# Fetching the rows of the attention heads quad by quad, and making the key parts two steps later

## The reference

```python
q = _apply_rope_full(x @ wq.T); k = _apply_rope_full(x @ wk.T); v = x @ wv.T
scores = jnp.einsum('bhqd,bhkd->bhqk', q, k) / math.sqrt(Dh)
scores = scores + _alibi_slopes(H)[None, :, None, None] * rel[None, None]
scores = jnp.where(causal[None, None], jnp.float32(-1000000000.0), scores)
out = jnp.einsum('bhqk,bhkd->bhqd', jax.nn.softmax(scores, axis=-1), v)
return out.transpose(0, 2, 1, 3).reshape(B, S, D) @ out_w.T + out_b
```

## Time and profile before

| | |
|---|---|
| median of 3 runs | 1346.04 us |
| the profiled execution | 1347.82 us |
| its span (first to last instruction) | 1346.0 us |
| mean granted clock of PE | 0.958 |
| busy: PE, DVE, ACT, POOL | 1223.6, 908.5, 641.6, 235.5 us |
| a_q loads of 512 KB, issue to landing | 4.2 us (8 of them) |
| a_k loads of 256 KB, issue to landing | 5.2 us (16 of them) |

### The profile page before, as it was taken

The page is one execution under the profiler, slowest core; times in us unless marked ns, Lnnn a source line. Parts: engine busy times, 40 slices in busy tenths (PEclk is TensorE's granted clock), DMA queues, the critical chain, the costliest instruction groups (busy, mean ns, idle before and its releaser), DMA issues.

```text
span 1346.0 us, 17205 instructions
## 1 busy us (share of the span) xinstructions
PE 1223.6 (91%) x6152; PEld 794.7 (59%) x6152; DVE 908.5 (67%) x1754; ACT 641.6 (48%) x1183; POOL 235.5 (17%) x201
## 2 busy tenths in 40 slices
PE   5998788899899889799999979789998997989998
PEld 3676444567666555466667744346676664556665
DVE  6765856455467698987765677564555677989765
ACT  4544344534323487862234325444433226969322
POOL 3001000000020065661000010000000101928210
PEclk9999879999999979799999999899999997979999
DMA  6213121000101121220200032200001012212120
GB/s 225 56 32 95 41 57 35 2 1 0 63 1 63 42 69 35 95 95 0 72 24 0 24 88 54 61 4 1 1 1 63 13 51 57 79 57 79 64 71 9
DMA packets 32581, 63.20 MB, mean 47 GB/s; under 512 B 4176, under 2 KB 19824, under 8 KB 32304
## 3 DMA queue, kind: packets, MB, share of 16 engines
q1 hardware_dynamic: 32496, 62.11, 14.7%
HBM read 54.16 MB, written 8.45 MB: 47 GB/s over the span
## 4 chain that ended last, share of the span: by engine, by line
PE 70%; DVE 12%; ACT 9%; DMA 3%; POOL 2%; issue 2%; SPq 1%; DVEq 0%; ACTq 0%; POOLq 0%
PE bank L1519 13%; PE bank L1520 12%; PE bank L1521 12%; PE bank L1688 9%; PE bank L1528 5%; PE bank L1834 3%; DVE a_mx L1400 3%; ACT n_part L1067 3%; PE bank L1597 3%; PE bank L1749 2%; PE bank L1658 2%; ACT n_da L1059 2%; POOL n_hc L819 2%; DMA a_k<-stack_dram 2%; PE bank L1724 2%
## 5 line engine op out<-in xcount | busy, mean ns | idle before, releaser
L1244 DVE SCALAR_TENSOR_TENSOR f_hl<-bank,f_hh 128x512 fp32r<-128x512 f32 x192 | 131.8, 689 | 130.4 <-ACT f_hh L893 129.7
L893 ACT ACTIVATE f_hh<-bank 128x512 fp32r<-128x512 f32 x192 | 114.7, 598 | 188.8 <-PE bank L1597 188.4
L955 ACT ACTIVATE m_sl<-bank 128x512 f32<-128x512 f32 x144 | 86.1, 599 | 235.2 <-PE bank L1521 234.8
L819 POOL TENSOR_TENSOR n_hc<-n_h,n_cs 128x512 f32<-128x512 f32 x128 | 159.9, 1278 | 179.0 <-DVE n_h L1490 172.6
L1519 PE MATMUL bank<-xT_h,mw_h 128*128 128x512 f32 x288 | 161.3, 560 | 3.5 <-DVEq L529 2.7
L1490 DVE TENSOR_TENSOR_SCAN n_h<-n_da,bank 128x512 f32<-128x512 f32 x128 | 149.9, 1207 | 10.0 <-PE bank L1528 7.2
L1688 PE MATMUL bank<-m_h,mw 128*128 128x512 f32 x288 | 145.6, 594 | 0.0
L1400 DVE TENSOR_REDUCE a_mx<-bank 128x1 f32<-128x384 f32 (+3 forms) x176 | 106.2, 637 | 52.6 <-PE bank L1789 50.2
L1311 DVE TENSOR_TENSOR m_t<-m_sl,bank 128x512 f32<-128x512 f32 x128 | 87.9, 687 | 78.4 <-PE bank L1521 77.3
L1834 PE MATMUL bank<-n_hc,ident 128*128 128x512 f32 x256 | 136.1, 619 | 0.2
L973 ACT ACTIVATE a_p<-bank 128x1024 f32<-128x1024 f32 (+3 forms) x128 | 87.8, 703 | 91.7 <-PE bank L1726 90.7
(11 more groups left out here) (241 smaller groups left out, 2362.7 us busy)
## 6 DMA issues: line engine op xcount, KB each, us to landing
n_cs<-c_dram SPq DMA_DIRECT2D x32, 512.0 KB, 3.6
m_c<-comb_dram SPq DMA_DIRECT2D x28, 512.0 KB, 5.1
a_q<-stack_dram SPq DMA_DIRECT2D x8, 512.0 KB, 4.2
a_k<-stack_dram SPq DMA_DIRECT2D x16, 256.0 KB, 5.2
stage_fw<-in_fw_dram SPq DMA_DIRECT2D x6, 512.0 KB, 7.0
stack_dram<-R SPq DMA_DIRECT2D x16, 192.0 KB, 2.8
w_stage<-in_mw_dram SPq DMA_DIRECT2D x9, 256.0 KB, 2.7
stack_dram<-R SPq DMA_DIRECT2D x16, 128.0 KB, 2.6
```

What stands on the lines that cost most here:

```text
L819: n_hcs.by(nc.gpsimd.tensor_tensor(n_hc[:, i % 4, :], n_h[:, i % 4, :], n_cs[:, j % C_RING, i // 2 % 2, :], ALU.mult))
L1244: f_lo.by(V.scalar_tensor_tensor(f_h[1][:, i % 4, :], bank[:, i % 3, :], 0.0, f_h[0][:, i % 4, :].bitcast(F32), ALU.max, ALU.subtract))
```

## The change

There are now three groups of transfers for the rows of the heads: the first half as before (group 0), the third quad (group 1) and the fourth quad (group 2), each with semaphores of its own. Every group is one load of queries and two of keys. In the first batch's unit SP fetches group 0 of the next batch behind the scores of step 15, then waits for the scores of step 23 (the third quad's last) and fetches group 1; group 2 comes behind step 31. Ahead of a stage the load of group 0's queries follows the key rows instead of going before them. On PE the first slot of the fourth quad waits for group 2. Inside the first batch's steps, stages 15 and above come two later: the key parts on ACT at steps 11, 12 and 13, the residuals on DVE at 11 and 12.

```diff
+KEYS_LATER = 2
@@ stage_at
+                if host == "mha":
+                    ahead = {n + KEYS_LATER * (n >= 15): name for n, name in ahead.items()}
                 return ahead.get(i)
@@ sync engine
-            def half_queries(k, n):
-
-                sp.wait_ge(a_wr.sem, a_wr.at(k, 5))
-                pairs = slice(4 * n, 4 * n + 4)
-                a_ldq[n].by(sp.dma_start(a_qs[n][:], stack_dram[0].rearrange("o r h t -> (o r) h t")[:, pairs]))
-
-            def half_keys(k, n):
-
-                sp.wait_ge(a_wr.sem, a_wr.at(k, 11))
-                pairs = slice(4 * n, 4 * n + 4)
-                for odd in range(2):
-                    a_ldk[n].by(sp.dma_start(a_ks[n][64 * odd:64 * odd + 64, odd::2], stack_dram[1, odd][:, pairs]))
+            def head_rows_in(k, n):
+
+                first, count = ((0, 4), (4, 2), (6, 2))[n]
+                to = slice(first % 4, first % 4 + count)
+                sp.wait_ge(a_wr.sem, a_wr.at(k, 5))
+                a_ldq[n].by(sp.dma_start(a_qs[first // 4][:, to],
+                                         stack_dram[0].rearrange("o r h t -> (o r) h t")[:, first:first + count]))
+                sp.wait_ge(a_wr.sem, a_wr.at(k, 11))
+                for odd in range(2):
+                    a_ldk[n].by(sp.dma_start(a_ks[first // 4][64 * odd:64 * odd + 64, odd::2][:, to],
+                                             stack_dram[1, odd][:, first:first + count]))
@@
-                        half_queries(k, 1)
-                        half_keys(k, 1)
+                        head_rows_in(k, 1)
+                        head_rows_in(k, 2)
                     for quad in range(QUADS):
                         if p == 0 and quad == 3:
 
                             sp.wait_ge(a_s2.sem, a_s2.at(k, NS2 // 2 - 1))
-                            half_queries(k + 1, 0)
-                            half_keys(k + 1, 0)
+                            head_rows_in(k + 1, 0)
+
+                            sp.wait_ge(a_s2.sem, a_s2.at(k, 3 * STEPS_4 - 1))
+                            head_rows_in(k + 1, 1)
                         sp.wait_ge(a_mok.sem, a_mok.at(k, quad))
@@
                             sp.wait_ge(a_s2.sem, a_s2.at(k - 1, NS2 - 1))
-                            half_queries(k, 1)
-                            half_keys(k, 1)
+                            head_rows_in(k, 2)
@@
-                    half_queries(k, 0)
                     head_rows(k, 1)
-                    half_keys(k, 0)
+                    head_rows_in(k, 0)
@@ tensor engine
-                    if n % (2 * NS1) == 0:
-                        rows_of_half(k, quad // 2)
+                    if n % NS1 == 0 and quad != 1:
+                        rows_of_quads(k, max(quad - 1, 0))
```

More of the change, by code:

```diff
@@ L438, in program @@
         a_wr = sig("a_wr", "mha", 12, 16)
-        a_ldq = [sig(f"a_ldq_{n}", "mha", 1, 16) for n in range(2)]
-        a_ldk = [sig(f"a_ldk_{n}", "mha", 2, 16) for n in range(2)]
+        a_ldq = [sig(f"a_ldq_{n}", "mha", 1, 16) for n in range(3)]
+        a_ldk = [sig(f"a_ldk_{n}", "mha", 2, 16) for n in range(3)]
         a_rld = sig("a_rld", "pair", 1, 16)
@@ L583, in head_rows @@
                 if k % 2 == 1:
-                    for n in range(2):
+                    for n in range(3):
                         sp.wait_ge(a_ldq[n].sem, a_ldq[n].at(k - 1, 0))
@@ L1751, in weigh_heads, with rows_of_quads @@
                 a_pv.by(ins)
-            def rows_of_half(k, n):
-                pe.wait_ge(a_fill.sem, a_fill.at(k // 2, 2 * n + 1))
+            def rows_of_quads(k, n):
+                pe.wait_ge(a_fill.sem, a_fill.at(k // 2, 1 if n == 0 else 3))
                 pe.wait_ge(a_ldq[n].sem, a_ldq[n].at(k, 0))
```

## The result

The changed kernel takes 1352.09 us, the median of 8 runs (1349.38 to 1355.25); the kernel before takes 1345.99 us in 8 runs (1345.21 to 1348.04). The ratio is 1.0041 with a 95% interval of 1.0032 to 1.0051: slower by 6.1 us. The profiled execution took 1352.11 us, with a span of 1350.3 us against 1346.0.

What follows compares the result with a forecast made beforehand. TensorE was taken as the bound, busy 1223.6 of 1346.0 us. Key parts −4.1, split −6.9, third quad's rows +16.4 make +5.4 us: 1351.4 us against the median of 1346.04, range 1345.5 to 1357 (own range 1348.5 to 1355).

Steps and rivals of the forecast that it cites:

- The signs that the prediction named: Step 24 idle 5 to 7 us, clock near 0.5 behind it; key stops 2 to 3 us; second half's stop gone.
- Third quad's rows behind step 23: SP's new wait ahead of the fourth quad's maxima: step 24 6.0 us later plus 2.2 slow clock, 16.4 us lost in all.
- the lower bound of 1.0 us: Bound for SP's one a_q and two a_k issues behind step 23, if half size issues faster; 1.7 was taken.
- The write behind the bulk: The small max_dram write behind the 512 KB rows is held up: 2.5 us until its loads, against 1.34 with an empty queue.
- The rival with a write not held up: At step 24 the max_dram write isn't delayed by the rows: 4.8 us lost per pair; total 1346.8 us, chance 0.16.
- Clock: PE's clock falls behind each new stop at step 24, costing 2.2 us more per pair, bounds 0 and 4.4.
- mostly paid back: Write not held up at step 24, slow phase 1.1 us on average: 11.8 lost, 11.0 gained, 1346.8 us; chance 0.16.
- Key parts: Two steps later, the stop between steps 8 and 16 goes: 2.8 us gained in pair 1, 1.3 in pair 2, together 4.1.
- The split: Fourth quad's rows alone behind step 31: stop for the second half goes, 2.46 us in pair 1, 4.46 in pair 2, together 6.9.
- Queries behind the key rows: Ahead of the stage, the first a_q load behind the six key-row writes: cost 0, bound 0.5 us per pair.
- the bulk is no faster for being half: Write ahead of step 24 waits nearly 7 us: 8.7 at step 24, 2.7 more per pair, 1356.8 us; chance 0.15.
- faster: PE's clock holds behind the key stop and at step 24: 15.4 gained, 9.6 lost, 1340.2 us; chance 0.12.

Runs made afterwards that it cites:

- experiment 1: Changed kernel with the wait for step 23 and the third quad's rows moved behind the fourth quad's maxima transfers: 1333.93 us, ratio 0.9912 to the kernel before.
- experiment 3: Changed kernel without the wait for step 23, third and fourth quad's rows both fetched behind step 31 in two groups: 1333.15 us.
- experiment 4: Changed kernel with the key parts back at their old steps: 1355.38 us.
- experiment 2: Changed kernel with the wait for step 23 left in place, the third quad's transfers issued behind the fourth quad's maxima: 1341.54 us.
- Experiment 7: Kernel of experiment 1 with the key parts one step later instead of two: 1334.24 us.
- experiment 6: Kernel of experiment 3 with the key parts at their old steps, so the split alone: 1340.62 us.
- Experiment 8: Kernel of experiment 1 with the first queries fetched ahead of the key rows again: 1334.37 us.

## Why the prediction was right, and what it had wrong

Forecast 1351.4, measured 1352.1. The mechanism is shown by more than the agreement of the sum: with the wait and its rows moved behind the two loads (experiment 1), the stop at step 24 is gone in both pairs and with it 18 us. The signs that the prediction named came too, the nearest to a miss being step 8 to 24 in pair 1, 32.1 us against its 33.3. That the total is 0.7 us off is partly luck: by the experiments the three terms are −5.7 (−3.3 within the change), −5.4 and +18.2, where the sum had −4.1, −6.9 and +16.4. (Its chances don't quite add up: 0.53 and 0.15 make 0.68, not 0.70.)

- **Third quad's rows behind step 23.** The forecast was 16.4 us. By rows it is 6.15 + 5.86 of stops and 1.85 + 1.57 of slow clock, 15.4; by the medians of the change and experiment 1 it is 18.2 (by the ratios 17.4), with about 2.4 us either way from the two intervals. The pieces: handover 0.31 (said 0.24), issues 1.64 (1.7), write 3.06 and 2.77 (2.5), loads to matmul 2.86 (3.15). The write was 0.3 to 0.6 us longer than said, the way from the loads to the matmul 0.3 shorter; these errors cancel. Half the bytes did not halve the issue time: two a_k issues of half size last 1.22 us against 1.28, so the lower bound of 1.0 us was no real case.
- **The write behind the bulk.** The Trainium skill ("DMA: Bandwidth & Descriptors", section "Queues, rings and completion order") has descriptors of one DMA engine consumed in order, and the semaphore's increment land only after that engine's earlier writes. The trace agrees: the write's loads could be issued 4.70 us after the bulk's first issue (191.78 to 196.48), where a group of that size takes 4.7 to 5.5 us by experiment 3; the changed kernel's 16 a_k loads of 128 KB land 3.6 us after their issue (median), which would be 196.4 for the last one here (an estimate from 192.77 + 3.6). All four writes right behind the rows took 2.75 to 3.06 us (the change and experiment 4), the two at the same place with nothing ahead 1.36 and 1.35 (experiment 2). The rival with a write not held up falls. The prediction's own evidence was weaker than it read: its 2.47 us followed the bulk, but in the same trace the write at 203.22 took 2.20 us (its loads went out at 205.42) with nothing issued for 10 us ahead of it. So how much of the 2.8 to 3.1 us the bulk makes is shown for this place alone: 1.4 to 1.7.
- **Clock.** It fell behind both new stops, worth 1.85 and 1.57 us, not 2.2. The rival "mostly paid back" had this at 1.1 us and the write not held up: the slow phases came out halfway between the two, the write was held up in full.
- **Key parts.** Forecast 4.1 us; 5.7 measured alone, 3.3 within the change. The stop between steps 8 and 16 went as said, its 3.39 us. In the trace, pair 1 gained 1.2 us more than forecast and pair 2 0.7 less, which cancel in part. Three things were off. Step 8 to 24 in pair 1 is 32.1 us, 1.2 under my 33.3, which I had from pair 2 with its slow phase: in the changed kernel's pair 1 the slow phase behind the keys is half as long. Its windows (184.13 and 847.16 are the first slots behind the keys):

```profile
184.30:187.70 3.40, 3.40 (x23) 1.48 (x22) 1.33 (x2) 0.00 (x0) 0.00 (x0) 0.57 0.02 5
187.70:191.00 3.30, 2.99 (x30) 1.58 (x28) 2.26 (x5) 1.19 (x2) 0.00 (x0) 1.00 0.00 0
...
846.50:853.30 6.80, 6.12 (x36) 3.27 (x36) 2.22 (x4) 1.15 (x2) 0.00 (x0) 0.53 0.00 0
```

  And a stop of 1.45 us that I hadn't named appears at 172.62, as VectorE waits 2.20 us for the second key part behind the values. Experiment 7 speaks against its costing anything. Timelines of ACT and then of DVE, changed kernel, pair 1:

```profile
166.80 0.64 ACT L885 ACTIVATE R<-xn 128x512 bf16<-128x512 f32 x1
...
170.12 0.60 ACT L998 ACTIVATE a_vs<-bank 128x512 f32<-128x512 f32 x1 [0.80 <-PE bank L1523]
170.61 0.62 ACT L885 ACTIVATE R<-xn 128x512 bf16<-128x512 f32 x1
```

```profile
171.27 0.69 DVE L1388 TENSOR_TENSOR xn<-xn,R 128x512 f32<-128x512 f32 x1 [2.20 <-ACT R L885]
```

  The first key part waits no longer (3.25 us in the earlier trace rows), as said. In pair 2 the change gave 0.6 instead of 1.3 us: the third quad's maxima, whose write had taken 1.34 us, took 2.45 (831.59 to 834.04), and held the key rows behind them.
- **The split.** Forecast 6.9 us, measured 5.4 alone. The stop for the second half went as said; a part of the 5.4 comes from the shorter stop between steps 8 and 16, which the prediction didn't have (experiment 6). Step 24 to the output takes 26.61 us without stops (experiment 1) against the 26.28 expected, 0.3 per pair of the difference, and the arrangement without the early wait keeps a third-quad stop of about 1 us (experiment 3); the interval of the ratio is 1.8 us either way.
- **Queries behind the key rows.** Said 0, at most 0.5 per pair. The stage of the changed kernel starts 3.04 and 2.71 us behind the start of the last matmul group ahead of it (128.38 to 131.42, 790.98 to 793.69), before 2.51 and 2.50 (128.93 to 131.44, 789.71 to 792.21): 0.5 and 0.2 later. Experiment 8 finds no gain from undoing it.

Of the two rivals on size, "the bulk is no faster for being half" falls by experiment 3 (4.7 to 5.5 us, not 6.9), and "faster" by the granted clock of 0.52 behind step 24.

Open: key stops differ between profiled executions whose program is the same up to there (2.29 and 3.09 us in the change, 1.18 and 1.70 in experiment 1, 1.95 and 1.70 in experiment 3), so 1.3 and 2.5 us of the difference between the change and experiment 1, which lie between steps 8 and 24, may be chance; one profile each can't tell. The changed kernel's runs also scatter more (5.9 us) than those before (2.8), with no cause found.

## What to carry to other kernels

In a queue that runs in order, ask of every wait that you add what stands behind it and when that is due: here a transfer with 16 us of room (in experiment 1 it goes out at 190.88 and its first slot comes at 206.86) was put in front of one that the next step needed at once. The same transfer behind the urgent one (experiment 1 or 3) turned 6.1 us lost into 12 us gained; 1333.2 us is the best version found. And a small write right behind a bulk transfer came about as late as the bulk did, so count the bulk's issue time and the time until it lands, not the write's own size. Last, when one profile is to explain a median, look where its execution lies among the others (experiment 2).

## What the runs showed of the hardware

- The time to issue a transfer on SP did not follow its size: two a_k loads took 1.22 us at half size and 1.28 at full, and the two small loads from max_dram (6 KB each) 1.51, the longest per transfer of these. Directly behind other issues the write's own issue took 0.56 us (193.42) against 0.31 (190.23 in experiment 2).
- The lower clock followed the stops of 2.89 and 2.84 us in experiment 2, and those of 2.29 and 3.09 us ahead of the keys in the change (0.57 in 184.30 to 187.70, 0.53 in 846.50 to 853.30). It followed a stop of 1.70 us too (experiment 1, 0.55 in 835.1 to 838), but not those of 2.46 us in the kernel before (1.00 in 212 to 218) and 2.06 us in experiment 6 (1.00 in 169 to 178), nor that of 1.45 us in the change (1.00 in 169 to 175). The length of the last stop alone doesn't tell whether the clock falls.
- Most writes to max_dram took 1.34 to 1.38 us until their loads were issued, those right behind 512 KB 2.75 to 3.06. But 2.0 to 2.6 us also came with nothing issued in the 5 us ahead: 2.45 at 831.59 in the change (the last row write having been issued by 826.5), 2.20 at 203.22 in the kernel before, 2.57 at 198.09 in experiment 1. Why is open.
